# A modulated two-layer block on one core: sums of zeros spread over TensorE's start, VectorE's small instructions ordered singly, and the orders of four engines redone

## The reference

```
h     = silu(noise_encoding(t) @ W1 + b1) @ W2 + b2           # 16 x 512
scale = (h @ Wsc + bsc)[:, None, :]                           # 16 x 1 x 256
shift = (h @ Wsh + bsh)[:, None, :]
def norm(v): m, s = mean and variance of v over the whole 256 x 256 of a sample
             return (v - m) * rsqrt(s + 1e-5) * gamma + beta  # gamma, beta: 256 x 256
y   = silu(scale * norm(x) + shift) @ W_in + b_in
out = silu(scale * norm(y) + shift) @ W_out + b_out + x
```

## Time and profile before the change

| | us |
|---|---|
| median of three runs | 85.39 |
| lowest and highest of them | 83.17, 85.62 |
| the profiled execution | 84.33 |
| its span, from the first to the last instruction | 82.4 |
| mean granted clock of TensorE over the span | 0.975 |

### The profile page before, as it was taken

The page is one execution under the profiler, slowest core; times in us unless marked ns, Lnnn a source line. Parts: engine busy times, 40 slices in busy tenths (PEclk is TensorE's granted clock), DMA queues, the critical chain, the costliest instruction groups (busy, mean ns, idle before and its releaser), DMA issues.

```text
span 82.4 us, 1277 instructions
## 1 busy us (share of the span) xinstructions
PE 76.9 (93%) x312; PEld 42.0 (51%) x314; DVE 66.3 (80%) x201; ACT 54.7 (66%) x169; POOL 49.1 (60%) x57
## 2 busy tenths in 40 slices
PE   4999779899999999999999999999999999999960
PEld 1346557567845454464555454444455545466620
DVE  1196298498999999999899998998979897995560
ACT  4113102199797899887988999888999799850000
POOL 3000574984989999999999999999703032100000
PEclk9999997599999999999999999999999999999998
DMA  1999999999400000031200240007600000066625
GB/s 26 361 326 354 438 391 419 407 403 414 181 10 0 0 4 0 0 127 51 81 0 8 87 168 0 0 0 274 236 4 0 0 4 0 0 255 255 229 97 184
DMA packets 4903, 11.92 MB, mean 145 GB/s; under 512 B 672, under 2 KB 1184, under 8 KB 4640
## 3 DMA queue, kind: packets, MB, share of 16 engines
q1 hardware_dynamic: 4464, 11.54, 36.5%
q10 hardware_dynamic: 432, 0.31, 1.2%
HBM read 7.65 MB, written 4.19 MB: 144 GB/s over the span
## 4 chain that ended last, share of the span: by engine, by line
PE 82%; DMA 10%; DVE 2%; SPq 1%; issue 1%
PE acc L808 31%; PE acc L828 30%; DMA x_sb<-x_dram 10%; PE acc L816 5%; PE acc L839 4%; PE acc L724 3%; PE acc L730 2%; PE stat_m L779 2%; DVE bn L494 2%; PE stat L791 1%; PE stat L758 1%; PE stat L764 1%; PE acc L736 1%; DVE o_sb L563 1%; PE stat_m L775 1%
## 5 line engine op out<-in xcount | busy, mean ns | idle before, releaser
L339 ACT ACTIVATE act<-act,cond 128x256 f32<-128x256 f32 x64 | 36.1, 593 | 5.0 <-DVE act L558 2.5
L808 PE MATMUL acc<-act,win_sb 128*128 128x512 f32 x56 | 27.3, 607 | 0.0
L828 PE MATMUL acc<-act,wout_sb 128*128 128x512 f32 x56 | 26.9, 602 | 0.0
L355 ACT ACTIVATE squares<-acc,shift 128x256 bf16<-128x256 f32 x32 | 14.7, 468 | 2.4 <-issue 1.8
L267 POOL TENSOR_TENSOR act<-act,gamma_sb 128x512 f32<-128x512 f32 x11 | 14.4, 1321 | 0.4
L828 PEld LDWEIGHTS acc<-act,wout_sb 128*128 128x128 f32 x56 | 10.1, 190 | 8.8 <-issue 7.9
L272 POOL TENSOR_TENSOR act<-act,beta_sb 128x512 f32<-128x512 f32 x11 | 13.9, 1280 | 0.6
L808 PEld LDWEIGHTS acc<-act,win_sb 128*128 128x128 f32 x56 | 9.9, 190 | 8.3 <-issue 7.3
L563 DVE SCALAR_TENSOR_TENSOR o_sb<-acc,const_sb,x_sb 128x512 f32<-128x512 f32 (+1 forms) x18 | 11.9, 686 | 2.6 <-PE acc L839 1.8
L551 DVE SCALAR_TENSOR_TENSOR act<-acc,shift,gamma_sb 128x256 f32<-128x256 f32 x32 | 13.9, 473 | 0.0
L251 POOL TENSOR_TENSOR rstd<-var,minus_half 128x2 f32<-128x2 f32 x8 | 6.5, 814 | 10.4 <-DVE var L517 10.4
(11 more groups left out here) (65 smaller groups left out, 66.0 us busy)
## 6 DMA issues: line engine op xcount, KB each, us to landing
x_sb<-x_dram SPq DMA_DIRECT2D x8, 512.0 KB, 12.4
out_dram<-o_sb SPq DMA_DIRECT2D x14, 256.0 KB, 2.0
w_sb<-w_dram SPq DMA_DIRECT2D x1, 1024.0 KB, 7.1
wss_sb<-wss_dram SPq DMA_DIRECT2D x1, 1024.0 KB, 10.1
w_sb<-w_dram SPq DMA_DIRECT2D x1, 256.0 KB, 2.8
gamma_sb<-gamma_dram SPq DMA_DIRECT2D x1, 256.0 KB, 8.1
beta_sb<-beta_dram SPq DMA_DIRECT2D x1, 256.0 KB, 10.3
win_sb<-w_in_dram SPq DMA_DIRECT2D x1, 256.0 KB, 10.5
```

The lines of the kernel that those rows point to most:

```text
L339: return nc.scalar.activation(buf[:, c, b], buf[:, c, b], ACT.Silu, bias=cond[:, 1, c, i:i + 1], scale=cond[:, 0, c, i:i + 1], **kw)
L355: nc.scalar.activation(squares[:, i % N_SQUARES], y_slot(p, c)[:, b], ACT.Square, bias=shift2[:, p, c, b:b + 1], accum_out=stat_in[:, p, B ...
L808: mm = nc.tensor.matmul(y_slot(p, c)[:].rearrange("p b s -> p (b s)"), win_sb[:, k, c * P:(c + 1) * P], act1[:, p, k].rearrange("p b s -> ...
L828: mm = nc.tensor.matmul(bank_of(("O", p, c, 0, BP))[:].rearrange("p b s -> p (b s)"), wout_sb[:, k, c * P:(c + 1) * P], act2[:, p, k].rear ...
```

## The change

It has four parts.

1. TensorE's start: the bias product (mean_b) goes ahead of everything but the eleven sums of zeros, mean1(0) ahead of the h1 product, mean1(1) ahead of the transposing product of h2, and there are 31 sums of zeros in all, where there were 26.
2. Small instructions of VectorE that had been pairs or groups in one function become calls of their own: `stats1_square` and `stats1_spread` out of `stats1_deviation`, `variance2_half` out of `variance2`, `add_sums` out of `weigh_sums`. Each can now stand anywhere in VectorE's list. In 12 places other work stands between two that depend on each other.
3. The lists of TensorE, VectorE, ScalarE and GpSimd, and the tables that go with them, are redone. Number and form of the matmuls of the two layers and of the statistics are the same.
4. Helpers that choose where a statistic's input and output lie (`columns_with_var2`, `in_stats`, `part_of`, `mean1_ps_of` and others). Their tables MEAN2_WITH_VAR2, MEAN1_WITH_VAR2 and RSTD1_WITH_RSTD2 are empty, and SPREAD_WITH_VAR2 equals the former SLOT_OF_STATS, so they give what there was before. The small results in the PSUM bank `stat` move to other columns, and var2 and rstd2 become parts of tiles `variance` and `rstd`.

The core of the diff:

```diff
-SLOT_OF_STATS = {3: 0, 4: 1, 5: 2, 6: 3, 7: 4}
+SPREAD_WITH_VAR2 = {3: 0, 4: 1, 5: 2, 6: 3, 7: 4}
+MEAN2_WITH_VAR2 = {}
+MEAN1_WITH_VAR2 = {}
...
+RSTD1_WITH_RSTD2 = {}
...
-SENT_BY_ACT = ((7, 0, 1, 1), (7, 1, 1, 1))
+SENT_BY_ACT = ((5, 1, 0, 2), (7, 0, 1, 1))
...
                 nc.vector.tensor_tensor(dev_ps[:], part_of(p)[:, :, 0], mean1_ps_of(p), ALU.subtract).then_inc(dev_ready, 1)
+
+            def stats1_square(p):
                 dve.wait_ge(dev_ready, 2 * (p + 1))
...
+            def stats1_spread(p):
                 dve.wait_ge(dev2_ready, p + 1)
...
+            def variance2_half(p):
+                dve.wait_ge(var2_mm, p + 1)
...
             def variance2(p):
                 dve.wait_ge(var2_half_ready, p + 1)
...
+            def add_sums(p):
                 dve.wait_ge(weighted_sum_ready, MEAN2_BY_SUMS.index(p) + 1)
```

GpSimd's list, at its start:

```diff
             layer1_rstd(1)
+            centre1(1, 1)
             weigh_beta(0, 1)
-            centre1(1, 1)
             weigh_gamma(1, 1)
             weigh_beta(1, 1)
```

VectorE's list, at its start (h2 is the add of L582):

```diff
             stats1(1)
-            dve.wait_ge(pads_set, 2)
-            dve.wait_ge(h2_mm, 1)
-            nc.vector.tensor_tensor(h2[:, :, 0:B], h2_ps[:, 0, 0:KH * B].rearrange("p (k b) -> p k b", k=KH),
...
             stats1_deviation(1)
+            stats1_square(1)
+            dve.wait_ge(pads_set, 2)
+            dve.wait_ge(h2_mm, 1)
+            nc.vector.tensor_tensor(h2[:, :, 0:B], h2_ps[:, 0, 0:KH * B].rearrange("p (k b) -> p k b", k=KH),
...
+            stats1_spread(1)
+            weigh_gamma(1, 0)
+            stats1_variance(1)
             weigh_gamma(0, 0)
-            stats1_variance(1)
-            weigh_gamma(1, 0)
             weigh_beta(0, 0)
```

TensorE's list, at its start and at its end:

```diff
             pe.wait_ge(consts_set, 1)
+            pe.wait_ge(const_in, 16)
+            for c in range(C):
+                mm = nc.tensor.matmul(stat_m[:, 0:1], mean_w[:], const_col(COL_BIN, c), start=(c == 0), stop=(c == C - 1))
+            mm.then_inc(mean_b_mm, 1)
+            warm(2)
+            mean1(0)
+            warm(1)
             pe.wait_ge(h0_ready, 1)
             pe.wait_ge(w1_in, 16)
             for n in range(KH):
                 mm = nc.tensor.matmul(h1_ps[:, 0, n * B:(n + 1) * B], w1_sb[:, n * P:(n + 1) * P], h0[:], start=True, stop=True)
             mm.then_inc(h1_mm, 1)
-            mean1(0)
-            warm(4)
+            warm(2)
             variance1(0)
+            warm(3)
             pe.wait_ge(h1_ready, KH)
             pe.wait_ge(w2_in, 16)
             rows_product(h2_rows_ps, h1, lambda k, j: w2_sb[:, k, j * P:(j + 1) * P]).then_inc(h2_rows_mm, 1)
-            warm(1)
+            warm(2)
+            mean1(1)
             pe.wait_ge(h2_rows_ready, 1)
             transposed(h2_ps, h2_rows).then_inc(h2_mm, 1)
-            pe.wait_ge(const_in, 16)
-            for c in range(C):
-                mm = nc.tensor.matmul(stat_m[:, 0:1], mean_w[:], const_col(COL_BIN, c), start=(c == 0), stop=(c == C - 1))
-            mm.then_inc(mean_b_mm, 1)
-            mean1(1)
-            warm(4)
+            warm(3)
             variance1(1)
             pe.wait_ge(h2_ready, 1)
             pe.wait_ge(wss_in, 16)
             rows_product(cond_rows_ps, h2, lambda k, j: wss_sb[:, k, j // C, (j % C) * P:(j % C + 1) * P]).then_inc(cond_rows_mm, 1)
-            warm(1)
+            warm(2)
             pe.wait_ge(cond_rows_ready, 1)
             transposed(cond_ps, cond_rows).then_inc(cond_mm, 1)
             warm(5)
...
+            layer2_last(1, 1, 0)
+            layer2(5, 1, 1)
             layer2_last(0, 1, 0)
-            layer2(5, 1, 0)
+            layer2_last(1, 1, 1)
             layer2_last(0, 1, 1)
-            layer2(5, 1, 1)
-            layer2_last(1, 1, 0)
-            layer2_last(1, 1, 1)
```

More of the change, by code:

```diff
@@ L77 @@
 MEAN2_BY_SUMS = (5, 6, 7)
-SENT_BY_ACT = ((7, 0, 1, 1), (7, 1, 1, 1))
+MEAN1_ALONE = tuple(p for p in range(NP) if p not in MEAN1_WITH_VAR2)
+VAR1_ALONE = tuple(p for p in range(NP) if p not in SPREAD_WITH_VAR2)
+MEAN2_ALONE = tuple(p for p in range(NP) if p not in MEAN2_WITH_VAR2)
+RSTD1_WITH_RSTD2 = {}
+RSTD1_ALONE = tuple(p for p in range(NP) if p not in RSTD1_WITH_RSTD2)
+SENT_BY_ACT = ((5, 1, 0, 2), (7, 0, 1, 1))
 N_SQUARES = 4
@@ L153, in build @@
         var2_half = sb("var2_half", [P, NP, BP])
-        var2 = sb("var2", [P, NP, BP])
-        rstd2 = sb("rstd2", [P, NP, BP])
+        variance = sb("variance", [P, NP, 2 * BP])
+        rstd = sb("rstd", [P, NP, 2 * BP])
         acc = [ps(f"acc{i}", [P, BP, S]) for i in range(ACCUMULATORS)]
@@ L198, in const_col, with columns_with_var2, in_stats, spread_of @@
             return const_sb[:, col + k:col + k + 1]
-        def spread_of(p):
-            if p in SLOT_OF_STATS:
-                return stat_in[:, SLOT_OF_STATS[p], C * BP:C * BP + BP]
-            return spread[:, BP * p:BP * (p + 1)]
+        def columns_with_var2(p):
+            at, end = {}, C * BP
+            for kind, table, width in (("spread", SPREAD_WITH_VAR2, BP), ("mean2", MEAN2_WITH_VAR2, BP),
+                                       ("part", MEAN1_WITH_VAR2, 2 * BP)):
+                for q in table:
+                    if table[q] == p:
+                        at[kind, q] = end
+                        end += width
+            return at, end
+        def in_stats(of, table, kind, q, width):
+            start = columns_with_var2(table[q])[0][kind, q]
+            cols = slice(start, start + width)
+            return stat_in[:, table[q], cols] if of == "sb" else stat[:, cols]
+        def spread_of(q):
+            if q in SPREAD_WITH_VAR2:
+                return in_stats("sb", SPREAD_WITH_VAR2, "spread", q, BP)
+            return spread[:, BP * q:BP * (q + 1)]
+        def var1_ps_of(q):
+            return in_stats("ps", SPREAD_WITH_VAR2, "spread", q, BP) if q in SPREAD_WITH_VAR2 else var1_ps
+        def part_of(q):
+            if q in MEAN1_WITH_VAR2:
+                return in_stats("sb", MEAN1_WITH_VAR2, "part", q, 2 * BP).rearrange("p (b t) -> p b t", t=2)
+            return part[:, BP * q:BP * (q + 1)]
+        def mean1_ps_of(q):
+            if q in MEAN1_WITH_VAR2:
+                return in_stats("ps", MEAN1_WITH_VAR2, "part", q, 2 * BP).rearrange("p (b t) -> p b t", t=2)[:, :, 0]
+            return mean1_ps
+        def mean2_in_of(q):
+            if q in MEAN2_WITH_VAR2:
+                return in_stats("sb", MEAN2_WITH_VAR2, "mean2", q, BP)
+            return mean2_in[:, q]
+        def mean2_ps_of(q):
+            return in_stats("ps", MEAN2_WITH_VAR2, "mean2", q, BP) if q in MEAN2_WITH_VAR2 else stat_m[:, 0:BP]
+        def var1_of(q):
+            return variance[:, RSTD1_WITH_RSTD2[q], BP:2 * BP] if q in RSTD1_WITH_RSTD2 else var1[:, BP * q:BP * (q + 1)]
+        def rstd1_of(q, b):
+            if q in RSTD1_WITH_RSTD2:
+                return rstd[:, RSTD1_WITH_RSTD2[q], BP + b:BP + b + 1]
+            return rstd1[:, BP * q + b:BP * q + b + 1]
         def bank_of(product):
@@ L287, in _ @@
             layer2_rstd(0)
+            centre1(3, 1)
             centre1(3, 0)
-            centre1(3, 1)
+            weigh_gamma(3, 1)
             weigh_gamma(3, 0)
-            weigh_gamma(3, 1)
+            weigh_beta(3, 1)
             weigh_beta(3, 0)
-            weigh_beta(3, 1)
             layer1_rstd(4)
@@ L519, in weigh_gamma @@
+                nc.vector.tensor_scalar(var1_of(p), var1_ps_of(p), EPS, None, ALU.add).then_inc(var1_ready, 1)
             def weigh_gamma(p, b):
```

461 lines of the change are left out of this document (253 added, 208 removed), and 22 rows, old and new, of tables (PRODUCTS, SQUARES, WEIGHTED).

## The result

The changed kernel is slower: its time is 1.0306 of before, 95% interval 1.0219 to 1.0392. Over six executions each, the medians are 86.51 us (85.38 to 89.6) and 84.69 us (83.17 to 88.91). The ratio is taken from the executions that lie within 1.5% of the fastest of each kernel. The profiled execution took 85.38 us, with a span of 83.6. The forecast was 83.2 us, and 85.4 was the end of its range.

What follows compares the result with a forecast made beforehand. It took TensorE to bound the 61.85 us main stage, behind a 17.66 us start chained through several engines. 84.33 - 1.3 (start) + 0.05 (sum of zeros) + 0.2 (given back) + 0 (tail) = 83.3, taken as 83.2; range 82.6 to 85.4.

Steps and rivals of the forecast that it cites:

- The clock: Start, 13 to 17 us: clock stays at 1.00, the 32 matmuls of wss_sb take 1.08 us in place of 1.91.
- The first product: End of TensorE's start: first product begins at 16.35 us in place of 17.66, a gain of 1.3 us.
- The w2 product: Condition's product in the start: begins at 9.5 us, between 8.87 and 10.4, at no cost.
- cover for h2's add and the three sums: Start, up to 13.3 us: waiting for transfers hides this added work, so it costs 0, at most 0.2 us.
- The tail: After TensorE's last product: no change, 0 us, bounds -0.1 and +0.1.
- the 0.05 for the second sum of zeros: Start, behind the 32 matmuls: two sums of zeros in place of one cost 0.05 us.
- The orders redone: Main stage: 61.85 us can't shrink; 0.2 us of the start's gain is given back, bounds 0 and 1.3.
- A: Rival, start: the clock falls all the same, 84.4 to 84.7 or 85.4 us; chance 0.22, shared with a no-effect rival.
- B: Rival, main stage: the start's gain of 1.3 us is all given back, 84.4 us; chance 0.12.
- C: Rival, from 13.3 us on: clock stays down into the products, slower, 85.6 to 87.3 us; chance 0.08.
- The step on the small instructions: VectorE's dependent small instructions ordered singly: 1.6 us of its time saved, worth 0 in kernel time, as slack.
- More runs are like the fast one, and hardly a faster fast one: Whole kernel: the change mostly spares runs the clock's fall; lowest timed run of before 83.17 us, forecast median 83.2.

Runs made afterwards that it cites:

- start_26: Kernel before with the change's TensorE and VectorE starts, but 15 sums of zeros after the first eleven, not 20: 0.9995 of before.
- start_both: Kernel before with the change's start of TensorE and VectorE's part of it, all later orders as before: 0.9987 of before.
- gamma2_late: Kernel before with only weigh_gamma(2, 0) moved behind stats1(3), where the change has it: 1.0295 of before.
- gamma_from_psum: Changed kernel with VectorE's weigh_gamma of blocks 2, 6 and 7 reading beta in PSUM in place of gamma in SBUF: 1.0043 of before.
- rest_only: Changed kernel with TensorE's list up to the first product as before (26 sums of zeros): 1.0351 of before.
- all_from_psum: Changed kernel with weigh_gamma of blocks 2, 6 and 7 reading beta in PSUM, and wsum in PSUM for wmean: 0.9937 of before.
- start_both_wsum: Kernel before with the change's TensorE and VectorE starts, and wsum in PSUM so that wmean reads PSUM: 0.9946 of before.
- pool_yields: Kernel before with both changed starts, wsum in PSUM, and two waits making GpSimd wait for VectorE's weigh_gamma(6, 0) and (7, 0): 1.0007 of before.
- gammas_back: Changed kernel with weigh_gamma(2, 0) moved ahead of stats1(3) and weigh_gamma(6, 0) to just before weigh_beta(6, 0): 1.0114 of before.
- start_only: Kernel before with only TensorE's list up to the first product from the change, VectorE's order as before: median 84.66 us against 83.7.

## Why the prediction was wrong

*Point by point.* The clock: right in its mechanism. It is 1.00 in the profile from 13 to 17 us, the 32 matmuls take 1.08 us, and start_26 shows that the added sums do it. The first product: forecast 16.35, measured 15.61 in this execution; with the transfer nearly as in before (9.94, start_both) it is 16.34, and 16.23 to 16.52 in six traces. That the mechanism there had one more part, b_in_c waiting for GpSimd, the forecast didn't have; that it still hit is in part luck. The w2 product was forecast to start at 9.5 and started at 9.64. The forecast's cover for h2's add and the three sums, the transfer of wss_sb, was absent here: the weights were there at about 11.95 (issued at 3.05, 8.9 us to land), and the product started at 12.56, directly behind the three sums (11.49 to 12.30) and variance1(1). What they cost was not tested by itself. The tail was put at 0, bounds -0.1 and +0.1. The span now ends 3.29 us after the last product and not 2.89: two sums on VectorE stand behind each other there (0.92 in the chain) where one stood (0.48). It is so in every trace with the change's end (3.2 to 3.3) against 2.8 to 2.9 with the old one. In the sum itself, the 0.05 for the second sum of zeros is counted twice, as 16.35 holds it already.

*The step that failed* is the term of "The orders redone": "Bounds for what is given back: 0, and 1.3 (TensorE tied wholly to an engine that did not move). ... I take 0.2." TensorE's two waits measured 1.83 + 0.96 = 2.8 us, more than twice the upper bound. Between the two profiled executions the whole closes as 84.33 - 1.89 (the first product) + 2.69 (first product to last, 64.70 against 62.01) + 0.40 (tail) - 0.15 (outside the span, 1.78 against 1.93) = 85.38. The bound assumed that each instruction keeps its length and that only places change. In fact the redone orders changed the lengths: weigh_gamma(2, 0), put behind stats1(3), and weigh_gamma(6, 0), put ahead of finish(1, 0), came beside GpSimd's passes and went from 0.75 to 1.80 and 2.84, and wmean, moved in time by the earlier start alone, from 0.28 to 1.16. The premise that from the first product on TensorE's own work is the chain failed with it: up to 24.36 us the chain is VectorE's. gamma2_late shows the first move by itself at 1.0295, and gamma_from_psum shows that the place is harmless if one operand is not in SBUF.

The trace of before had the sign. centre1 took 1.29 us beside weigh_gamma and otherwise 0.77, and rstd 1.15 and otherwise 0.70. The 1.15 was taken as the length of that instruction, and the prediction has no term for what the two engines do to each other. The section on the chip says that the streams meet only at semaphores; in these traces they meet at their access to SBUF as well.

*The rivals.* A (the clock falls all the same) did not happen in the profile; four of the six executions of the changed kernel have a mean clock of 0.977 to 0.981. Where in them the clock fell was not traced; rest_only shows one way, behind the wait of 2.99 us. B (given back in the main stage) had the right place and the wrong size: it allowed 1.3 and no more, and gave as its reason how busy the engines were, not that single instructions get longer. C (slower) had the right sign with 0.08, and the wrong mechanism. The step on the small instructions was not tested by itself: no run singles them out without the redone orders. all_from_psum, with 61.85 us from first to last product against 62.01, leaves them and the orders together at most a few tenths.

*The start's worth.* "More runs are like the fast one, and hardly a faster fast one" holds for start_both: 0.9987 by the ratio, with the clock up in all of 10. Its median over all executions, 83.86 against 83.81, shows no gain. My reading is that what the clock gives is spent on wmean's 0.8 us and on executions in which passes collide. The second rests on the spread and on one profiled case (start_both_wsum) and is not shown for each execution.

*Left open.* Why block 1's statistics start anywhere from 8.97 to 10.58 us; what the executions of before at 86.6 to 88.9 us are, of which some have a mean clock of 0.997 or 1.00 and others of 0.94, and none was traced; and why pool_yields has a ratio 0.6% above the kernel without its waits, with intervals that overlap.

## What to carry to other kernels

An instruction's length from a trace holds for what ran beside it. Before an instruction of VectorE that reads two tensors from SBUF, or a TENSOR_SCALAR that reads and writes SBUF as wmean and b_in_c do, is moved, look at what GpSimd does at the new place, and look in the trace of before for the same operation at two lengths: 1.29 beside 0.77 was the warning. Where it can't be placed safely, put one operand into PSUM, or let GpSimd wait for it by a semaphore; moving it by hand exchanged one collision for another here (gammas_back).

## What the runs showed of the hardware that was not expected

VectorE can lose the port several times in a row: it stood through two of GpSimd's passes (2.84 us) and through four (4.87 us) when these followed each other without a gap, and ended 0.54 to 0.55 us after the last. Even an instruction of two columns is hit: b_in_c, 128 x 2, takes 0.23 us alone (start_only), 0.26 in before, where GpSimd's pass was nearly over, 0.73 in start_both beside the pass from 10.96 to 12.23, and 1.27 in gamma_from_psum:

```profile
10.96 1.27 POOL L267 TENSOR_TENSOR act<-act,gamma_sb 128x512 f32<-128x512 f32 x1
11.52 0.73 DVE L591 TENSOR_SCALAR b_in_c<-const_sb,mean_b 128x2 f32<-128x2 f32 x1
```

```profile
10.97 1.27 DVE L659 TENSOR_SCALAR b_in_c<-const_sb,mean_b 128x2 f32<-128x2 f32 x1
```

It stands ahead of the condition: in gamma_from_psum block 1's statistics start 0.23 us later than in the changed kernel's trace (9.39 and 9.16), and the first product 0.72 later (16.33 and 15.61).

And a wait of TensorE of 2.99 us in the middle of dense work was followed by a fall of its clock to 0.50 (rest_only, 59 to 60 us), so that one collision can cost twice. The wait of 1.83 us in the changed kernel left it at 1.00.
